# Cross-attention and feed-forward kernel on one core: the opening starts with K's units instead of Q's

## The reference, cut to what matters

```python
x = x + L0_xattn(layernorm(x), ctx)       # 16 heads of 64: q from x, k and v from ctx, softmax, @ Wo + bo
x = x + L0_ffn(layernorm(x))              # a shared feed-forward and one of two experts per token
x = x + L1_xattn(layernorm(x), ctx, ctx)  # one head, masked query rows
x = x + L1_ffn(layernorm(x))              # int8 product with a scale for the whole of x

def L0_xattn(x, ctx):
    q, k, v = x @ Wq, ctx @ Wk, ctx @ Wv  # 256 -> 1024, split into 16 heads
    attn = softmax(einsum('bihd,bjhd->bhij', q, k) * SCALE)
    return einsum('bhij,bjhd->bihd', attn, v).reshape(b, n, 1024) @ Wo + bo
```

## Time and profile before

| | us |
|---|---|
| median of three runs (1011.4 to 1012.23) | 1011.82 |
| the profiled execution, its own time | 1010.56 |
| its span, from the first to the last instruction | 1008.8 |
| PE busy | 952.8 (94%) |
| DVE busy | 630.7 (63%) |
| ACT busy | 494.3 (49%) |
| POOL busy | 233.7 (23%) |
| mean granted TensorE clock of the span | 0.976 |

### The profile page before, as it was taken

The page is one execution under the profiler, slowest core; times in us unless marked ns, Lnnn a source line. Parts: engine busy times, 40 slices in busy tenths (PEclk is TensorE's granted clock), DMA queues, the critical chain, the costliest instruction groups (busy, mean ns, idle before and its releaser), DMA issues.

```text
span 1008.8 us, 20313 instructions
## 1 busy us (share of the span) xinstructions
PE 952.8 (94%) x6876; PEld 842.2 (83%) x6876; DVE 630.7 (63%) x1606; ACT 494.3 (49%) x1198; POOL 233.7 (23%) x296
## 2 busy tenths in 40 slices
PE   5889999999999999999999999889999999999764
PEld 4768889888988988898889889778988888988643
DVE  6856665665665666656656657659564665664557
ACT  4655555565565565555655655434233323334133
POOL 0323323332432333233323323310000000000204
PEclk9999999999999999999999999989999999999975
DMA  9200000000000000000000000022401202102102
GB/s 299 81 8 17 0 15 15 0 15 0 15 15 0 15 15 0 15 15 0 15 1 14 15 0 1 1 84 93 122 1 50 73 0 65 58 1 77 46 1 73
DMA packets 20077, 33.63 MB, mean 33 GB/s; under 512 B 1616, under 2 KB 16496, under 8 KB 19040
## 3 DMA queue, kind: packets, MB, share of 16 engines
q1 hardware_dynamic: 20048, 33.25, 10.7%
HBM read 31.41 MB, written 1.84 MB: 33 GB/s over the span
## 4 chain that ended last, share of the span: by engine, by line
PE 90%; DVE 6%; ACT 2%; issue 1%; DMA 0%; POOL 0%; DVEq 0%; ACTq 0%
PE bank L1237 26%; PE bank L1405 12%; PE bank L1471 12%; PE bank L1266 9%; PE bank L1285 8%; PE bank L1251 7%; PE bank L1219 6%; PE bank L1306 5%; PE bank L1434 2%; PE bank L1454 2%; PE bank L1207 1%; PE bank L1313 1%; DVE norm_stats L734 1%; PE bank L1442 1%; PE bank L1418 1%
## 5 line engine op out<-in xcount | busy, mean ns | idle before, releaser
L460 POOL TENSOR_TENSOR probs<-probs,row_rcp 112x375 f32<-112x375 f32 x256 | 202.7, 814 | 431.1 <-DVE row_rcp L807 431.0
L550 ACT ACTIVATE probs<-bank,neg_max 112x375 f32<-112x375 f32 x256 | 144.7, 571 | 70.0 <-DVE neg_max L801 68.6
L659 ACT ACTIVATE hid<-bank,b_col 128x448 f32<-128x448 f32 x96 | 61.1, 636 | 160.3 <-PE bank L1471 158.0
L1266 PE MATMUL bank<-ident,probs 112*125 112x112 f32 x768 | 129.8, 279 | 4.8 <-DVE probs_t L812 4.8
L1266 PEld LDWEIGHTS bank<-ident,probs 112*125 112x125 f32 x768 | 114.9, 189 | 21.8 <-issue 6.1
L801 DVE TENSOR_REDUCE neg_max<-bank 112x1 f32<-112x375 f32 x256 | 123.4, 540 | 9.5 <-PE bank L1251 9.5
L812 DVE COPY probs_t<-bank 125x336 f32<-125x336 f32 x128 | 64.7, 506 | 72.2 <-PE bank L1266 68.0
L1023 DVE CAST hid_hi<-hid 128x448 fp32r<-128x448 f32 x96 | 37.7, 393 | 100.0 <-ACT hid L659 99.2
L1237 PE MATMUL bank<-ctx_hi,wk_hi 128*128 128x376 f32 x256 | 97.5, 381 | 2.7 <-DVE k_parts L792 1.5
L522 ACT ACTIVATE k_parts<-bank 128x376 fp32r<-128x376 f32 x128 | 62.2, 486 | 70.2 <-PE bank L1237 70.2
L792 DVE TENSOR_TENSOR k_parts<-bank,k_parts 128x376 fp32r<-128x376 f32 x128 | 69.9, 547 | 37.1 <-ACT k_parts L522 36.9
(11 more groups left out here) (150 smaller groups left out, 1990.2 us busy)
## 6 DMA issues: line engine op xcount, KB each, us to landing
ctx_raw<-in_ctx_t SPq DMA_DIRECT2D x16, 375.0 KB, 3.3
stage<-in_ffn_up SPq DMA_DIRECT2D x3, 1024.0 KB, 4.7
stage<-in_ffn_down SPq DMA_DIRECT2D x3, 1024.0 KB, 6.8
stage<-in_ctx_t SPq DMA_DIRECT2D x8, 375.0 KB, 4.7
stage<-in_ctx_n SPq DMA_DIRECT2D x8, 375.0 KB
ring_more<-in_ctx_t SPq DMA_DIRECT2D x8, 375.0 KB, 6.4
ring_more<-in_ctx_n SPq DMA_DIRECT2D x8, 375.0 KB
x_all<-in_x SPq DMA_DIRECT2D x1, 1344.0 KB, 14.7
```

What stands on the lines that cost most here:

```text
L460: eng.tensor_tensor(probs[s][:, :], probs[s][:, :], row_rcp[:, s:s + 1].broadcast_to([S, C]), ALU.mult).then_inc(probs_ready, 1)
L550: eng.activation(probs[r][:, :], SCORE_BANKS[i][0:S, 0:C], ACT.Exp, bias=neg_max[:, r:r + 1], accum_out=row_sum[:, r:r + 1]).then_inc(exp_ ...
L1266: t = eng.transpose(turn_bank(i, project)[0:CJ, j * S:(j + 1) * S], probs[QUAD * v + i][:, j * CJ:(j + 1) * CJ], ident[0:S, 0:S])
```

## The change

The order of the opening is another one on four engines, and the counters follow it.

- SP: x is no longer first. The context and K's first weights are, then one batch of x (`x_all[:, 0:1]`), V's first weights, Wq's first half, and only then batches 1 to 3 of x. x has three semaphores instead of two.
- PE: units in the order K, K, K, K, V, Q, V, V, by number 1, 2, 3, 4, 5, 0, 7, 6 (`FIRST_UNITS`); the transposes of the first batch's tokens stand between the last K and the first V.
- ACT: its parts in the same order, with the rounding of the other weight pieces in between.
- DVE: the remainders of context and weights first; the 13 norm steps of batch 0 are spread over the time of the first K units (6, then 3, then 4), and the norms of batches 1 to 3 stand behind all its parts of Q and K.
- `unit_count` and `hi_count` count along the new order for half 0, and the first scores also wait for Q's remainder.

```diff
--- before.py
+++ after.py
@@ -203,7 +203,7 @@
         result = [r[0:S, 0:GB * D] for r in ring]
 
 
-        x_loaded = [sem(f"x_loaded{i}") for i in range(2)]
+        x_loaded = [sem(f"x_loaded{i}") for i in range(3)]
         small_loaded = sem("small_loaded")
         bo_loaded = sem("bo_loaded")
         ws_loaded = sem("ws_loaded")
@@ -312,12 +312,23 @@
 
             return bank[1] if isinstance(g, int) and g == 0 else bank[5]
 
+
+        FIRST_UNITS = (1, 2, 3, 4, 5, 0, 7, 6)
+
+        def first_half(f):
+
+            return isinstance(f, int) and f == 0
+
         def unit_count(f, k):
 
+            if first_half(f):
+                return sum(i % 2 == k % 2 for i in FIRST_UNITS[:FIRST_UNITS.index(k) + 1])
             return 4 * f + k // 2 + 1
 
         def hi_count(f, k):
 
+            if first_half(f):
+                return sum(i < V_UNIT for i in FIRST_UNITS[:FIRST_UNITS.index(k) + 1])
             return 5 * f + k + 1
 
         def halves(b, last):
@@ -365,18 +376,19 @@
                 half = slice(512 * c, 512 * c + 512)
                 eng.dma_start(wq_sb[:, :, half], wq[:, :, half]).then_inc(wq_loaded[c], 16)
 
-            eng.dma_start(x_all[:, 0:GB, :], x[:, 0:GB, :]).then_inc(x_loaded[0], 16)
             eng.wait_ge(consts, 1)
             eng.dma_start(ctx_raw[:, :, 0:C], ctx_t[0]).then_inc(ctx_loaded, 16)
             load_piece(0)
+            eng.dma_start(x_all[:, 0:1, :], x[:, 0:1, :]).then_inc(x_loaded[0], 16)
+            load_piece(1)
             load_wq(0)
-            load_piece(1)
+            eng.dma_start(x_all[:, 1:GB, :], x[:, 1:GB, :]).then_inc(x_loaded[1], 16)
             load_piece(2)
             load_wq(1)
             eng.dma_start(bo_row[:, :], bo.rearrange("(a n) -> a n", a=1).broadcast_to([S, D])) \
                .then_inc(bo_loaded, 16)
             load_piece(3)
-            eng.dma_start(x_all[:, GB:B, :], x[:, GB:B, :]).then_inc(x_loaded[1], 16)
+            eng.dma_start(x_all[:, GB:B, :], x[:, GB:B, :]).then_inc(x_loaded[2], 16)
             eng.wait_ge(ctx_split, 1)
             eng.dma_start(ctx_raw[:, :, 0:C], ctx_t[1]).then_inc(ctx_loaded, 16)
             eng.dma_start(wo_sb[:, :, :], wo).then_inc(wo_loaded, 16)
@@ -589,15 +601,18 @@
 
             round_ctx(0)
             piece_hi(0)
+            unit(0, 1, 0)
+            piece_hi(1)
+            unit(0, 2, 0)
+            unit(0, 3, 0)
             tokens_out(0, 0, heads_bank[0])
-            piece_hi(1)
-            for k in range(4):
-                unit(0, k, 0)
+            unit(0, 4, 0)
+            unit(0, 5, 0)
             piece_hi(2)
-            unit(0, 4, 0)
+            unit(0, 0, 0)
+            unit(0, 7, 0)
             piece_hi(3)
-            for k in range(V_UNIT, 8):
-                unit(0, k, 0)
+            unit(0, 6, 0)
             batch(0, first=True)
             with eng.Fori(1, B - 1) as b:
                 batch(b)
@@ -774,11 +789,14 @@
                                          norm.rstd[:, bass.ds(j, 1)], ALU.subtract, ALU.mult) \
                           .then_inc(xn_ready[which], 1)
 
+            ctx_rest(0)
             eng.wait_ge(x_loaded[0], 16)
-            norm_batches(norm1, 0, 0, 1)
-            normalise(0, norm1, 0, 0, xn[0])
-            ctx_rest(0)
+            norm_stats(norm1, 0, 0)
             piece_lo(0)
+            eng.wait_ge(norm1.step, 1)
+            norm_moments(norm1, 0)
+            for i in range(6):
+                norm_op(norm1, 2, i, slice(0, 1))
 
             def unit_lo(f, k, cf):
 
@@ -908,7 +926,7 @@
 
                 base, rest = 2 * GB + 2 * NORM_OPS, B - GB
                 if n == 1:
-                    eng.wait_ge(x_loaded[1], 16)
+                    eng.wait_ge(x_loaded[2], 16)
                 if 1 <= n <= 6:
                     for b in range(GB + (n - 1) * rest // 6, GB + n * rest // 6):
                         norm_stats(norm1, b, b)
@@ -922,13 +940,21 @@
                 if n == 13:
                     eng.wait_ge(norm1.step, base + 2 * rest + NORM_OPS)
 
+            unit_lo(0, 1, 0)
+            for i in range(6, 9):
+                norm_op(norm1, 2, i, slice(0, 1))
+            unit_lo(0, 2, 0)
+            for i in range(9, NORM_OPS):
+                norm_op(norm1, 2, i, slice(0, 1))
+            eng.wait_ge(norm1.step, 2 + NORM_OPS)
+            normalise(0, norm1, 0, 0, xn[0])
+            unit_lo(0, 3, 0)
+            piece_lo(1)
+            unit_lo(0, 4, 0)
+            unit_lo(0, 0, 0)
+            piece_lo(2)
+            eng.wait_ge(x_loaded[1], 16)
             norm_batches(norm1, 2 + NORM_OPS, 1, GB - 1)
-            unit_lo(0, 0, 0)
-            unit_lo(0, 1, 0)
-            piece_lo(1)
-            for k in range(2, V_UNIT):
-                unit_lo(0, k, 0)
-            piece_lo(2)
             piece_lo(3)
             batch(0, first=True)
             with eng.Fori(1, B - 1) as b:
@@ -1240,6 +1266,8 @@
 
             def quad_scores(visit, u, c, v):
 
+                if first_half(u):
+                    eng.wait_ge(proj_used[Q_UNIT % 2], unit_count(u, Q_UNIT))
                 for k in (K_UNIT + 2 * v, K_UNIT + 2 * v + 1):
                     eng.wait_ge(proj_used[k % 2], unit_count(u, k))
                 if positive(visit):
@@ -1362,15 +1390,16 @@
                             turn_tokens(1, b - 1, TOKENS_BANK)
 
             eng.wait_ge(consts, 3)
-            turn_tokens(0, 0, heads_bank[0])
-            eng.wait_ge(wq_loaded[0], 16)
-            unit(0, 0, 0, 0)
             eng.wait_ge(weights_split, 1)
             for k in range(K_UNIT, V_UNIT):
                 unit(0, k, 0, 0)
+            turn_tokens(0, 0, heads_bank[0])
             eng.wait_ge(weights_split, 2)
-            for k in range(V_UNIT, 8):
-                unit(0, k, 0, 0)
+            unit(0, V_UNIT, 0, 0)
+            eng.wait_ge(wq_loaded[0], 16)
+            unit(0, Q_UNIT, 0, 0)
+            unit(0, V_UNIT + 2, 0, 0)
+            unit(0, V_UNIT + 1, 0, 0)
             batch(0, first=True)
             with eng.Fori(1, B - 1) as b:
                 batch(b)
```

## The result

The changed kernel takes 1015.35 us (median of ten runs, 1013.97 to 1016.42) against 1011.97 us of the kernel before, run beside it. The ratio is 1.0038, 95% interval 1.0029 to 1.0046: slower by 2.9 to 4.7 us, 3.4 by the medians. The forecast was 1015.3 with 3.5 us of loss. The profiled execution took 1016.25 us with a span of 1014.5; that of the kernel before 1010.56 with 1008.8. So the two traces are 5.7 us apart, more than the medians, and the account has to say where the rest comes from.

A forecast was written before the change was run, and what follows sets the result against it. The time at which DVE can take the first maximum was held to set the clock of everything behind it. +2.4 us for DVE's queue and +1.1 for PE's clock gave +3.5: 1015.3 us on the median, range 1012.5 to 1017.2.

The forecast's parts named there:

- DVE's queue behind Q: DVE between its half of Q and the first maximum: work moved there makes that maximum 2.4 us later, 27.15 not 24.75.
- POOL's add of bo: POOL, waiting for the first normalised batch, now at 14.2: listed among everything else that costs nothing.
- nothing takes the 2.4 us back: DVE from first maximum to turned probabilities at 34.39: work without a gap, so the 2.4 us delay stays whole.
- The 30.85 of the prediction: Second K unit of the second half: PE waits some 4 us for DVE's half of Q, placed at 30.85.
- the earlier scores don't help: First scores on PE: 1.4 us earlier, at 22.5, but DVE takes the first maximum only 4.6 us after they begin.
- The clock: PE's granted clock behind its 4 us wait near 31 us: falls to half speed, costing 1.1 us, bounds 0 and 1.7.
- The case of a clock that holds: PE's clock stays up through the 4 us wait; only DVE's 2.4 us remain, 1014.2 us; chance 0.22.
- The clock is kinder elsewhere: PE's 1.7 us clock loss after 70.78 is not repeated: 1012.5 us, or 1013.6 with the loss near 31; chance 0.14.
- the sum of 3.5: Whole kernel: +2.4 us for DVE's queue and +1.1 for PE's clock, so 1010.56 becomes 1014.1, or 1015.3 on the median.
- The late loads: K's first weights land at 7.65 and not 5.8, everything to the first maximum 1.9 us later: 1017.2 us; chance 0.08.
- one batch of x fits behind them: Opening loads: 112 KB of x behind K's weights arrive before needed, as ACT rounds the weights meanwhile.
- The distance behind 35 us: Timeline after PE's restart and clock fall: a constant distance to the kernel before; shrinking after 35 us would prove it wrong.

The follow-up runs named there:

- the filled-wait profile: Changed kernel with 15 extra matmuls on PE behind the first K unit of the second half, against the kernel before: 1015.14 us, ratio 1.0027.
- the last version above: Changed kernel with norms of batches 1 to 3 before Q's remainder, batch 0's statistics behind K's remainder, V parts earlier: 1010.86 us, ratio 0.9997 to the kernel before.
- the first experiment: Changed kernel with DVE's norms of batches 1 to 3 moved before Q's remainder: 1011.25 us, ratio 0.9998 to the kernel before; second time 1012.0, 1.0007.
- experiment 4 with 30 matmuls: Changed kernel with 30 extra matmuls on PE behind the first K unit of the second half: 1017.17 us, ratio 1.0055 to the kernel before.

## Why the prediction was right

**DVE's queue behind Q: right, and the larger term.** Forecast +2.4 us, measured 3.0 in the profile and 2.6 in the second one (27.77 and 27.31 against 24.75). From Q's half to the first maximum I had 6.75 us; it was 6.72. What I had too small was its start, 21.05 and not 20.4. K's first matmul came at 8.69 and not 8.15, because K's weights were there at 6.28 and not 5.8; the context was half a microsecond late too (3.9 us from its issue and not 3.3), but ACT, done with it, still waited 0.68 us for the weights. Of this 0.3 us are left at DVE's half of K3 (14.91 and not 14.6). The rest is V's remainder, 1.58 us and not 1.22, beside POOL's add of bo, which the move of the normalising had brought there and which I had put down as costing nothing. Timeline of POOL:

```profile
15.15 0.72 POOL L462 TENSOR_TENSOR x_all<-x_all,bo_row 112x256 f32<-112x256 f32 x1 [13.00 <-DVE xn L788]
```

I had one step wrong here: "nothing takes the 2.4 us back". Between the first maximum and 27.81 DVE had been idle for 0.99 us in the kernel before, so its work was not without a gap: ACT's half of Q began there 1.89 us behind the first exponential (25.33 to 27.22), just when PE's Q unit ended (27.19), and in the changed kernel 1.66 us behind it (28.34 to 30.00), with PE long done. That gives a quarter of a microsecond back, hidden in the 1.0 of the first fall of the clock. (The 30.85 of the prediction is PE's restart, measured 31.26; DVE's half of Q was at 30.58.)

**That the earlier scores don't help: right.** Scores at 23.32 and not at 22.5, but the experiments say the same from both sides: with the norms moved back the loss is gone, with the norms moved alone it appears in the old order.

**The clock: right in kind, its size not settled.** Forecast 1.1, measured 1.04 and 0.37 in two profiles against the kernel before, 1.3 and 0.65 against the same stretch with the clock held (7.55). My picture was that it falls after PE's restart; in the first profile it fell inside the wait, in the second after it. The wait itself was 3.65 us against "some 4".

**The chances.** The case of a clock that holds did not come in either profile. "The clock is kinder elsewhere" was the wrong way round: the second fall, near 75 us, was 6.8 us long in both profiles of the changed kernel and 3.4 in that of the kernel before. I had argued from one trace, which showed only the shorter of two lengths. The other profiles do not tie the length to the change: with the norms late in the old order it was 3.4 us, with the new loads in the old order 6.8, with the old loads in the new order 3.4. That the sum of 3.5 meets the measured 3.4 to a tenth is partly luck: in the one trace the terms make 4.1 at 36 us, in the other 2.9, and each is uncertain by half a microsecond or more from run to run.

**The late loads** did not come in the form I had priced (weights at 7.65), but there is a smaller form: DVE waits for batch 0 of x, third in the queue of loads, ahead of K's remainder, and in the filled-wait profile that wait was 1.81 us and put K's start to 9.83. My step "one batch of x fits behind them" held in the two profiles of the changed kernel (no wait, and 0.55 us), and not in that one. Over seven profiles with this order of loads and statistics, the start of batch 0's statistics spreads by 1.8 us (6.36 to 8.18); K's weights were there between 5.99 and 6.84. The Trainium skill's statement on completion order (DMA: Bandwidth & Descriptors, Queues, rings and completion order), that a later DMA may complete before an earlier one, I had set beside the landing of the weights; no run here shows it, as in all twelve profiles the first loads, up to Wq's first half, landed in the order of issue.

**The distance behind 35 us** stayed at 4.1 us up to 74, as forecast, and then grew to 5.4, which I had not written down for the changed kernel.

## What to carry to other kernels

Ask which engine is last at the first synchronising step, and then look at what is queued in front of that step on that engine, not at who starts first: here PE's start came 1.7 us earlier and the end 3.4 us later, because 3.9 us of statistics and small norm steps had moved from beside PE's work to behind the last thing that DVE had to wait for. Work without a deadline belongs into the wait in front of a late operand, not behind it; moving one block there was worth 3.3 us in the trace. And put an operand that is needed later behind, not ahead of, the one that starts the chain, in the waiting engine's program too: in the last version above, with batch 0's statistics behind K's remainder, K began at 8.67, against 8.42 to 9.83 in the seven profiles with the statistics ahead of it. One profile does not show how often that helps.

## What the runs showed of the hardware that I had not expected

- TensorE's granted clock fell to one half (1.2 of 2.4 GHz) behind or within PE's waits of 1.6 to 3.65 us, but not behind all of them, and not in the same place from kernel to kernel: after the same 1.6 us wait, which ends between 41 and 48 us, it fell in three of the profiles (both of the first experiment and the new loads in the old order) and stayed at 1.00 in the others. Behind the wait near 70 us it was at half for 3.4 us in five profiles and for 6.8 us in seven, with the same wait of 3.54 to 3.64 us in front of it. That is 1.3 us of the time, as large as the effects measured here, and may go some way to explain why ten runs of one kernel lie 2.5 us apart: in two of three sets of runs of the kernel before the slower executions have the lower mean clock (correlation −0.74 and −0.76), in the third hardly (−0.24). What decides where it falls, and for how long, no run shows.
- In the first 4 us of PE's work the matmuls come at half pace (0.31 us from start to start of a K matmul, against 0.17 later), while the granted clock of those windows reads 1.00.
- A DVE instruction of 112x3 elements takes 0.16 us, and 0.61 to 0.81 when a POOL product or sum is running. For a large one (V's remainder, 128x1024) beside POOL's add of bo it was the one that began second that paid, in all seven profiles where they meet: where POOL began first (four profiles) DVE took 1.58 to 1.73 us instead of 1.22 and POOL its usual 0.72; where DVE began first (three) DVE took its 1.22 and POOL 1.37 to 1.77. Timeline of experiment 4 with 30 matmuls:

```profile
15.09 1.22 DVE L739 TENSOR_TENSOR wv_lo<-stage,wv_hi 128x1024 fp32r<-128x1024 f32 x1
15.14 1.76 POOL L462 TENSOR_TENSOR x_all<-x_all,bo_row 112x256 f32<-112x256 f32 x1 [12.99 <-DMA bo_row<-in_bo]
```

- The context's landing, nothing ahead of it, took 3.9 us from issue in the changed kernel's profile and 3.6 or 3.7 in the other eight with the new loads, while the median of all 16 is 3.3 in the kernel before.
